# Adding two of a state's four row tiles to y with one accumulating transfer instead of two GpSimd additions

## The reference

```python
h = layernorm(x) * (1 + ca) + sa
# mixer, inside it h is normalised by its RMS
xi, z = split(h @ in_proj.T)                 # 512 + 512 channels
u = silu(causal_conv4(xi))
dt, B, C = split(u @ x_proj.T, [16, 32])     # 16, 16, 16
delta = softplus(dt @ dt_proj.T + dt_b)      # 512 channels
for l in positions:                          # 16 states per channel
    s = s * exp(delta[l] * A) + delta[l] * B[l] * u[l]
    y[l] = sum_over_states(s * C[l])
y = (y + u * D) * silu(z)
x = x + ga * (y @ out_proj.T + h)
# experts: 16 routed (the best 4 per position, weights normalised), one shared of width 256
h = layernorm(x) * (1 + cb) + sb
x = x + gb * (shared(h) + sum_over_experts(w_e * expert_e(h)))
```

## Time and profile before

| | |
|---|---|
| median of three runs | 3052.31 us (3052.0 to 3054.66) |
| the profiled execution's own time | 3054.61 us |
| its span, first to last instruction | 3052.8 us |
| busy: DVE, POOL, PE, PEld, ACT | 84%, 84%, 82%, 65%, 60% |
| mean granted TensorE clock | 0.912 of full speed |
| transfers issued | all by SP; 187.97 MB in all |

### The profile page before, as it was taken

How to read it: one execution, slowest core, us unless ns; L and a number is a source line. 1 busy time by engine, 2 the same in 40 slices (tenths; PEclk the granted TensorE clock), 3 DMA queues, 4 the chain that set the end, 5 groups by cost and what they waited for, 6 DMA issues and landing times.

```text
span 3052.8 us, 52878 instructions
## 1 busy us (share of the span) xinstructions
PE 2488.1 (82%) x16524; PEld 1983.2 (65%) x16524; DVE 2568.1 (84%) x3986; ACT 1830.3 (60%) x3484; POOL 2563.1 (84%) x2379
## 2 busy tenths in 40 slices
PE   2566988879888797988879798887979888797979
PEld 0344766757676675767667576776757667576767
DVE  3579899888898988889898888889888898988953
ACT  2666666666666665665657566665656656665531
POOL 1689898989989898998989889898988989898942
PEclk7557998999999998999989899999989999999989
DMA  1311111211112111121112111121212211111101
GB/s 64 107 56 58 64 56 64 71 57 61 56 61 72 62 61 53 60 68 64 63 52 77 56 60 59 64 66 55 74 41 73 68 56 60 60 58 58 67 32 49
DMA packets 62150, 187.97 MB, mean 62 GB/s; under 512 B 12040, under 2 KB 14728, under 8 KB 61488
## 3 DMA queue, kind: packets, MB, share of 16 engines
q1 hardware_dynamic: 61872, 184.58, 18.0%
HBM read 166.68 MB, written 17.87 MB: 60 GB/s over the span
## 4 chain that ended last, share of the span: by engine, by line
POOL 29%; PE 27%; DVE 17%; issue 16%; ACT 9%; DVEq 1%; POOLq 1%; ACTq 0%; DMA 0%
POOL db_sb L639 12%; PE bank_ps L1236 9%; DVE states L995 7%; POOL y_sb L651 6%; PE moe_ps L1251 6%; PE rows_ps L1178 5%; POOL act L681 3%; POOL y_sb L659 2%; PE bank_ps L1160 2%; ACT da_ps L839 2%; DVE y_sb L1014 2%; DVE bank_ps L950 2%; DVE act L1089 1%; PE bank_ps L1134 1%; POOL du_sb L628 1%
## 5 line engine op out<-in xcount | busy, mean ns | idle before, releaser
L639 POOL TENSOR_TENSOR db_sb<-du_sb,b_sb 128x512 f32<-128x512 f32 x1024 | 1296.6, 1275 | 0.1
L1178 PE MATMUL rows_ps<-ident,states 128*128 128x128 f32 x4096 | 673.2, 295 | 163.7 <-DVE states L995 94.3
L651 POOL TENSOR_TENSOR y_sb<-y_sb,c_rows 128x512 f32<-128x512 f32 x512 | 655.1, 1280 | 169.8 <-ACT c_rows L817 169.8
L839 ACT ACTIVATE da_ps<-delta,a_sb 128x512 f32<-128x512 f32 x1024 | 701.8, 687 | 85.7 <-DVE states L995 84.2
L1178 PEld LDWEIGHTS rows_ps<-ident,states 128*128 128x128 f32 x4096 | 535.3, 153 | 281.9 <-DVE states L995 133.0
L1251 PE MATMUL moe_ps<-eout_sb,act 128*128 128x256 f32 x2304 | 627.7, 396 | 85.2 <-POOL act L681 83.5
L1236 PE MATMUL bank_ps<-h2T_high,ein_w_high 128*128 128x256 f16 x2304 | 644.0, 280 | 21.8 <-DVE delta L971 12.0
L995 DVE TENSOR_TENSOR_SCAN states<-da_ps,carry,db_sb 128x512 f32<-128x512 f32 x512 | 648.4, 1274 | 15.0 <-ACT da_ps L839 13.2
L1236 PE MATMUL bank_ps<-h2T_high,ein_w_low 128*128 128x256 f16 x2304 | 643.1, 279 | 0.0
L1236 PE MATMUL bank_ps<-h2T_low,ein_w_high 128*128 128x256 f16 x2304 | 642.4, 279 | 0.0
L995 DVE TENSOR_TENSOR_SCAN states<-da_ps,db_sb 128x512 f32<-128x512 f32 x512 | 616.2, 1213 | 23.2 <-ACT da_ps L839 13.0
(11 more groups left out here) (156 smaller groups left out, 2851.1 us busy)
## 6 DMA issues: line engine op xcount, KB each, us to landing
b_sb<-b_dram SPq DMA_DIRECT2D x128, 512.0 KB, 3.6
w_sb<-w_dram SPq DMA_DIRECT2D x128, 512.0 KB, 4.0
th_p<-x_dram SPq DMA_DIRECT2D x16, 512.0 KB, 5.8
r_dram<-conv SPq DMA_DIRECT2D x16, 512.0 KB, 2.6
x<-r_dram SPq DMA_DIRECT2D x16, 512.0 KB, 3.8
out_dram<-x SPq DMA_DIRECT2D x32, 256.0 KB, 2.2
mod_p<-mod_dram SPq DMA_DIRECT2D x8, 384.0 KB, 6.2
x<-e_in_dram SPq DMA_DIRECT2D x5, 512.0 KB, 4.6
```

What stands on the lines that cost most here:

```text
L639: pool.tensor_tensor(db_sb[:, n % NDB, :], du_sb[:, slots[t][0][0], b, :], b_sb[:, k % NBPAIR, s % BPAIR, :], ALU.mult).then_inc(sem["scal ...
L651: pool.tensor_tensor(place, place, c_rows[:, n % NCR, :], ALU.add).then_inc(sem["c_added"], 1)
L839: ac.activation(da_ps[n % NDA][:, :], delta[:, slots[t][0][0], b, :], ACT.Exp, scale=a_sb[:, b, s:s + 1]).then_inc(sem["exp_done"], 1)
L1178: last = pe.transpose(rows_ps[j % 2][:, b * P:b * P + P], states[:, step % 2 * NB + b, j * P:j * P + P], ident[:, :])
```

## The change

Rows 1 and 3 of a state (the position groups j = 1 and j = 3) are no longer added by GpSimd's arithmetic. ScalarE writes both scaled tiles side by side into one entry of `c_rows`, and one transfer with an add as its operation moves both (128 partitions, 2 rows of 512 values, 512 KB) onto `y_sb`. The transfer is issued from GpSimd's queue. It waits for the second of the two tiles and for the transfer of the state before (`c_added` now counts 16 for each transfer). `c_rows` becomes a ring of two states (four tiles where there were three), and the ring `db_sb` goes from 6 to 5 tiles. `y_gate` of groups 1 and 3 waits for the landing of the transfer of state 15, where it waited for the additions. The table `SHIFT` has new values for 29 kinds of step, and `SOFT` moves by 0.035 tick.

```diff
-NDA, NDB, NCR = 2, 6, 3
+NDA, NDB, NCR = 2, 5, 2
...
-            out += [(at + 0.145, ("c_scale", t, s, j)), (at + 0.892, ("c_add", t, s, j))] if j in C_ACT else [(at + 0.156, ("gather", t, s, j))]
+            out += [(at + 0.145, ("c_scale", t, s, j)), (at + 0.892, ("c_add", t, s))][:1 + (j == C_ACT[-1])] if j in C_ACT else [(at + 0.156, ("gather", t, s, j))]
...
-SOFT = 45.462
+SOFT = 45.427
...
-         "router": 1.67, "rows": 0.41, ... "x1": 0.99, "x1_norm": 0.93, ... "y_evac": 0.69, "y_gate": -0.15, "y_t": 0.99, "z": -0.23,
+         "router": 1.67, "rows": 0.41, ... "x1": 0.69, "x1_norm": 0.93, ... "y_evac": 0.39, "y_gate": -0.15, "y_t": 0.69, "z": -0.44,
...
-        c_rows = sb("c_rows", [P, NCR, DI])
+        c_rows = sb("c_rows", [P, NCR, len(C_ACT), DI])
...
-                    def c_add(t, s, j):
+                    def c_add(t, s):
 
                         step = NS * nS(t) + s
-                        n = len(C_ACT) * step + C_ACT.index(j)
-                        pool.wait_ge(*c_scales(step, j))
-
-                        pool.wait_ge(sem["c_added"], max(0, n - len(C_ACT) + 1))
+                        pool.wait_ge(*c_scales(step, C_ACT[-1]))
+
+                        pool.wait_ge(sem["c_added"], 16 * step)
                         if s == 0 and t > 0 and slots[t - 1][1] is not None:
                             pool.wait_ge(*bank_read(("skip_t", t - 1, NB - 1)))
-                        place = y_sb[:, slots[t][0][0], j, :]
-                        pool.tensor_tensor(place, place, c_rows[:, n % NCR, :], ALU.add).then_inc(sem["c_added"], 1)
+                        pool.dma_start(y_sb[:, slots[t][0][0], C_ACT[0]:NJ:C_ACT[-1] - C_ACT[0], :], c_rows[:, step % NCR, :, :],
+                                       accum_op=ALU.add).then_inc(sem["c_added"], 16)
...
-                            pool.wait_ge(*((sem["c_added"], nS(t) * NS * len(C_ACT)) if j in C_ACT else (sem["gathered"], nS(t) * NS * len(C_DVE))))
+                            pool.wait_ge(*((sem["c_added"], nS(t) * NS * 16) if j in C_ACT else (sem["gathered"], nS(t) * NS * len(C_DVE))))
...
-                        n = len(C_ACT) * step + C_ACT.index(j)
                         ac.wait_ge(sem["rows_full"], NJ * step + j + 1)
-                        ac.wait_ge(sem["c_added"], max(0, n - NCR + 1))
-                        ac.activation(c_rows[:, n % NCR, :], rows_ps[j % 2][:, :], ACT.Copy,
+                        ac.wait_ge(sem["c_added"], 16 * max(0, step - NCR + 1))
+                        ac.activation(c_rows[:, step % NCR, C_ACT.index(j), :], rows_ps[j % 2][:, :], ACT.Copy,
                                       scale=xd_sb[:, slots[t][0][0], j, AT_C + s:AT_C + s + 1]).then_inc(sem["c_scaled"], 1)
```

More of the change, by code:

```diff
@@ new lines @@
+SHIFT = {"b_load": 0.39, "b_store": 0.49, "c_add": 0.79, "c_scale": 0.59, "delta": -0.77, "dt_bias": 0.09, "du": -0.32, "e_act": -0.12,
+         "e_mul": -0.12, "e_tanh": -0.35, "e_weigh": 0.65, "ein_load": 0.17, "ein_low": 0.44, "eout_fold": 0.63, "eout_load": -0.11,
+         "exp": 0.87, "expert_in": -0.12, "expert_out": 0.65, "gather": 0.59, "h2_high": 0.21, "h2_low": 1.04, "h_rms": -0.31,
+         "h_scale": -0.62, "h_square": -0.36, "hn_high": -0.93, "hn_low": -0.62, "hn_t": -0.65, "logit_exp": 0.21, "op": 0.69,
+         "op_gate": 0.69, "out_add": -0.12, "out_gate": -0.21, "out_store": 0.38, "r_add": 3.69, "r_gate": -0.15, "r_store": 0.35,
+         "router": 1.67, "rows": 0.41, "scaled": -0.1, "scan": -0.15, "skip": -1.61, "skip_evac": -0.34, "skip_t": -0.32, "soft_exp": -0.4,
+         "soft_ln": 0.93, "tap": 0.14, "u": -0.55, "u_tanh": -0.55, "w_evac": 0.99, "w_load": -0.12, "w_t": 0.94, "x1": 0.69,
+         "x1_norm": 0.93, "x1_rstd": -0.41, "x1_stat": 0.69, "x_load": -2.41, "x_rstd": -0.61, "x_scale": 0.42, "x_stat": 0.15,
+         "xd_t": -0.08, "xd_t_evac": 0.27, "y_evac": 0.39, "y_gate": -0.15, "y_t": 0.69, "z": -0.44, "z_gate": -0.51, "z_tanh": -0.45}
```

## The result

The changed kernel took 3082.44 us (median of 3 runs, 3081.4 to 3083.69) against 3052.31: a ratio of 1.0097, 95% interval 1.0074 to 1.012. It is 1% slower. I had forecast 3017 us, that is, faster.

A forecast was written before the change was run, and what follows sets the result against it. No engine bounds the whole; GpSimd sets the pace in the late stretch. 15 slots x (4.1 gained - 1.5 lost) = 39 us, less 4 at the end, gives 35: 3017 us against 3052.3, range 2995 to 3040.

The forecast's parts named there:

- the relief: GpSimd loses 32 additions a slot, 40.60 us of its time, 16.18 us of it in the late stretch.
- the late stretch: From 1461 to 1521 in slot 8, where GpSimd is busy 59.32 of 60 us; forecast gain 4.1 us a slot.
- the 0.97: Late stretch: TensorE, next to set the pace, works at 0.97, so its 54.19 us take 55.9.
- c = 1.3 us: Cost on GpSimd's queue of issuing one transfer a state; ends taken were 0.32 and 4.7 us.
- the dear issue: Rival: issuing costs as much as the additions in GpSimd's late stretch; at c = 3.0 us, 3172 us; chance 0.20.
- L = 5.8 us: Landing time of a 512 KB transfer, making y_gate of group 1 4.4 us late at the slot's start.
- I charge 1.5 us, a third: Start of the slot: of the gate's 4.4 us delay only 1.5 us is lost; ends 0 and 4.4.
- Two idle places: Slack after the late gate: 1.1 us before L663 and 4.1 us before the router, taking up some delay.
- Edits at nothing: No cost charged for the wait for the previous state's transfer, both rings, SP's transfers and the new table.
- three signs of being wrong: Issue gaps over 2.3 us, L over 9 us, or w_t's wait for the router growing over 2 us a slot.
- A landing of 9 us or more: Rival: c small but the landing long, so the gate is 7.6 us late; 3060 to 3092 us; chance 0.12.
- the other three: Forecast cases: more relief 2940 us, chance 0.15; costly issue 3172 us, 0.20; no change 3045 to 3058 us, 0.13.

The follow-up runs named there:

- gate_order: The changed kernel with the mix stage taking the groups of rows in the order 0, 2, 1, 3: 3005.07 us, ratio 0.9836.
- old_table: The changed kernel, all states by transfer, with the table of the kernel before: 3079.44 us, ratio 1.0079.
- last_adds: The changed kernel with state 15 added by two GpSimd additions, states 0 to 14 still by transfer: 3029.74 us, ratio 0.9923.
- before_order: The kernel before with the mix stage taking the groups of rows in the order 0, 2, 1, 3: 3049.72 us, ratio 0.9992.
- best: The changed kernel with the old table, additions for all states in slot 1, transfers elsewhere, groups in order 0, 2, 1, 3: 3000.05 us, ratio 0.9822.

## Why the prediction was wrong

- **What bounds the kernel, and the relief: right.** 4.1 us a slot were forecast for the late stretch; the traces show 3.3 (scan of state 15 to the next slot: +4.67 to +1.40, and -0.11 to -3.40 in gate_order), 3.1 with the old table. It sits in the last 20 us. The engine next in line did not reach the 0.97 that I gave it: in the last 22 us VectorE has 20.78, 0.94.
- **c = 1.3 us: right.** The issue's record in the late stretch of the kernel after is 1.21 us long, and the record behind it starts 0.78 us after it, which looks like a cheaper issue:

```profile
1489.04 1.21 POOL L649 DMA_DIRECT2D y_sb<-c_rows  x1
1489.82 1.74 POOL L628 TENSOR_TENSOR du_sb<-delta,u_sb 128x512 f32<-128x512 f32 x1
1491.05 1.73 POOL L639 TENSOR_TENSOR db_sb<-du_sb,b_sb 128x512 f32<-128x512 f32 x1
```

  But the records behind it are 1.74 and 1.73 long where such an instruction took 1.27 before: they start early and end when the work is done. The semaphores show the cost. An operation over 128x512 directly behind an issue signals its end 2.48 us after the operation ahead of the issue did (median of 109 such places in the kernel after); two such operations with nothing between are 1.23 apart. That leaves 1.25 us for the issue. The rows of gate_order above say the same: issue, gate and `scaled` end at 1689.08, 3.72 us after 1685.36, and 3.72 - 2 x 1.23 = 1.26. At 1.25 the dear issue, from 2.26 on, is refuted. GpSimd's busy time fell by 312 us and not by the 655 that I named, because the page does count GpSimd's own issues as busy, 345.7 us for the 256, other than I wrote there and ahead of it.
- **L = 5.8 us: right, 5.6.** Over the 16 landings of state 15 it is 5.1, and the gate was 3.95 us late, forecast 4.4. By the Trainium skill's fit ("DMA: Bandwidth & Descriptors", section Anatomy of one DMA — SWDGE (gpsimd) path), an estimate of 3.2 us for 512 KB, the wait would have been 1.8; the measured landing decides.
- **The step that failed: "I charge 1.5 us, a third".** Two idle places were to take up most of the delay, 1.1 us ahead of x1_rstd and 4.1 ahead of the router. The first did take up 1.0 us (x1_rstd began 1.09 us after the last statistic, and now 0.09). But the delay had grown from 3.95 to 5.07 before it, with TensorE at half clock, so x1_rstd was still 4.06 late; with the old table it took up 0.4. The router took up nothing: it starts 4.03 to 4.10 us behind `logit_exp` in every one of the 14 slots, before and after alike, and both are 3.92 late. The gates of groups 2 and 3 stand behind the blocked one in GpSimd's queue, and their transposes and projections follow them. And what I took for slack at the router was VectorE's own queue, late by as much, since VectorE too had stood in the window above (15.75 instead of 20.76 us).

  At w_t the delay was 4.93, about 1.0 of it lost inside the router with the new table; with the old one (old_table) it was 3.63, and 4.07 at state 15. So 3.6 to 4.9 us passed on where I charged 1.5, more than the relief of 3.1 to 3.3. last_adds, gate_order and before_order show the size from three sides: 53, 77 and 0 us.
- **A row misread.** I let TensorE wait 7.0 us at w_t "for the router". The row names `u_sb` L960, an instruction of VectorE that ended 2.4 us after the router's last one (1385.12 and 1382.69) and stands behind it in VectorE's queue. A late router does delay TensorE, but by way of that queue.
- **Edits at nothing: the ring yes, slot 1 and the transfer before no.** I counted 15 slots and left the first out. It loses 8.7 us through blocked VectorE instructions; of these I had no term. The table costs 22 us beside additions, but beside transfers 3 or less, so in this sum it is 0 to 3. The wait for the transfer of the state before was not covered everywhere: in the kernel after GpSimd stood 29.8 us for it, in 18 waits. In slot 8 two issues stand 7.2 us apart (1391.32 and 1398.54) and not the 11.1 of a mean state. What this costs no run shows; in best there is no such wait.
- **Signs that kept silent.** None of my three signs of being wrong came: c is under 2.3, L under 9, and TensorE's longest wait ahead of w_t grew only from 7.3 to 8.2 us (means of 14 slots). All that stands behind the late gate moved with it, so a wait further down says little of the delay. The wait of PE L1251 for the weighing was to nearly go; it halved, 83.5 to 43.3 us.
- **Sums.** The slot of 178.3 us ran from a first gate to the fourth of the last slot; from first gate to first gate a full slot is 179.2. The upper end of the range, 3040, does not come out of its terms either: a gain of 1.8 against a wait halfway to 4.4 is 15 x (1.8 - 2.95) - 4 = -21, so 3074. The measured time lies above that too.
- **Put right**, the sum is 15 x (3.3 - 4.9) = -24 and -9 for slot 1: 3085 us, where 3082.44 was measured. As the terms are read from the kernel after itself, this closes the account and tests nothing.
- **The rivals.** A landing of 9 us or more was the one whose time (3060 to 3092) held the result. That is luck: L was as forecast, and it was the share that passes on that made the kernel slower. The measured time lies outside those of the other three.

What stays open: why the new table costs 22 us beside additions. A part can be seen: 1.1 us are lost each slot between the router's exponential and w_t (-0.74 to +0.35 against before), where its TENSOR_SCALAR takes 22.8 us in all instead of 11.2. Open too is how much of the loss is the clock's and how much the wait's own.

## What to carry to other kernels

When an operation is turned into a transfer, count its landing and not its issue alone; here most of what the landing cost came where the next step needs the result at once. Look for the one instance in each period that stands directly ahead of its reader, and move independent work (here another group of rows) between the two before counting a gain. Do not take slack off a delay at the head of a chain unless the trace shows that its stages don't wait for each other; idle time at the far end may be another engine's queue that gets late by the same amount. And look at the granted clock behind each wait of TensorE: in this kernel the new one was paid a second time, at half clock.

## What was not expected of the hardware

- An accumulating transfer of 512 KB within SBUF costs GpSimd's queue 1.25 us and lands after 5.6 us (median of 256), while two additions over the same data took 2.5 us of GpSimd. The records behind an issue start early (0.78 us after it) and are drawn out from 1.27 to 1.74 us; the semaphores give the right times.
- After some 3.5 us of waiting in two pieces (2.41 and 1.12) eight matmuls took 3.78 us instead of 1.97, at a granted clock of 0.50. This came in all 16 slots, and in 6 of them the level stayed for a second group.
- VectorE instructions that began behind a run of GpSimd's grew from 0.30 to 2.88 us and from 1.20 to 4.96; where VectorE began first, GpSimd's grew from 1.28 to 2.30. Taking one such instruction away moved the block to the next (median 0.225 to 0.907 us).
